# An attention and routed-FFN layer: GpSimd's program follows a planned order, the maxima are turned right behind their split, and the head-term scratch has another layout

## The chip, the cores and the metric

The kernel runs on one core of a Trainium2 chip. Time is device microseconds (us) of one execution, median over several runs; lower is better. Engines: PE (TensorE, matmuls), DVE (VectorE), ACT (ScalarE), POOL (GpSimd) and SP (SyncE, which here issues every DMA).

## What is computed

Input x is 4 batches (B) of T = 1024 tokens of D = 256 values. Both branches read the same layer-normalised x, and their results are added to x:

```python
xn = _layernorm(x)
x = x + attn(xn) + ffn(xn)

# attn: 16 heads of 16 values, causal
q, k, v = split_heads(xn @ Wq.T + bq), split_heads(xn @ Wk.T + bk), split_heads(xn @ Wv.T + bv)
q, k = rope(q), rope(k)
att = where(tril, einsum('bhqd,bhkd->bhqk', q, k) / 4, -inf)
y = softmax(att) @ v                 # then y @ Wo.T + bo
# ffn: 16 blocks of 64 hidden units, each token keeps the 4 blocks with the highest router score
h = relu(einsum('nd,ibd->nib', xf, w1b) + b1b), zero outside the 4 blocks
y = h @ w2.T + b2
```

## The kernel before

**Tiling.** Heads are taken in 16 groups (GROUPS; group n is batch n // 4, four heads each). A group's scores come in 12 units of 128 keys by up to 512 queries, for each of the 4 heads. Everything that PE makes goes through seven rotating PSUM banks (`banks`); the eighth (`o_bank`) holds the sums of probability times value.

**Precision.** Queries and keys are float32, cut into three bfloat16 pieces (high, mid, low). Six products of pieces (NTERM) times 16 values make 96 rows, the "stack" `q_st`/`k_st` of a group. A piece lies with heads on partitions, a stack with terms and values on partitions, so SP writes the pieces to DRAM (`term_scratch`, lines 587 to 621) and reads them back as stacks (lines 607 to 634). Three stacks rotate.

**Maxima.** For each row of scores PE first makes the scores once for their maximum ("max", line 1043), DVE reduces them (lines 1311 and 1314), and for each half of the queries of a group GpSimd cuts the negated maxima into three pieces ("split", `split_maxima`, lines 797 to 806). PE then transposes them ("maxT", the turn, line 1050), DVE copies the result (line 1323), and SP writes it to DRAM and loads it as three extra rows of `q_st` (`place_maxima`, lines 643 and 645). The scores proper ("score", lines 1102 and 1105) of that half need these rows; ACT takes their exponential (line 919). So each half of a group goes: last max on PE, DVE, split on GpSimd, turn on PE, DVE, two DMAs, first score.

**Rotation of queries and keys.** For batch 0 the first two of four projections (r = 0, 1) are rotated and cut by DVE and ACT (lines 1252 to 1275). All later ones, "chains" (b, r), are GpSimd's: `rotate_and_split` issues seven operations of 128x1024 (sin, cos, add, high, rest, mid, low; lines 749 to 776). `high` waits until the pieces of the chain before on the same buffers have been stored. GpSimd also adds the output bias to the accumulator tile (`add_biases`, line 812) and normalises x of the next batches (line 783).

**Order.** Each engine runs its own list in order and waits on semaphores. The lists of PE, ACT and DVE come from one planner (`arrange`): it keeps a clock in matmul columns and models when banks come free and when ACT and DVE are ready. It doesn't model GpSimd in the kernel before. There the turn of a half is placed by a count of maxima (`turned_maxima`, line 125: 24 maxima after the last of a first half, 12 after that of a second), and its scores a fixed 24,000 columns after the last max was read. GpSimd's list is written out by hand (lines 827 to 856), with whole chains between the splits. SP's list is by hand as well (lines 669 to 741).

**The start.** DVE normalises x of batch 0, then copies the value bias, spread over 128 columns, into `bv_wide` (line 1410) and makes the first rotations. GpSimd fills the constant rows of `k_st` (line 819). The first stack load needs all pieces of the first four heads of r = 0 and 1 in DRAM; the pieces of the other heads are stored after it (`store_other_pieces`, line 604), and the second stack load, of group 1, waits for these.

## Time and profile before

| what | us |
|---|---|
| median of 3 runs (lowest, highest) | 854.6 (854.21, 854.64) |
| the profiled execution | 853.66 |
| its span from first to last instruction | 851.9 |
| PE busy in that span | 816.7 |
| DVE, ACT, POOL busy | 591.8, 426.9, 281.6 |

The profile is of one execution. "Busy" of PE counts the time in which any matmul is in flight, so it isn't the share of its peak. A view's "idle before" is the time in which an engine had nothing to run ahead of an instruction, and the arrow names what ended it.

### The profile page before, as it was taken

Reading aid. Unit: us, or ns where it says so; the run is one execution under the profiler, and the core shown is the slowest. Engines: PE = TensorE matmul, PEld = TensorE weight load, DVE = VectorE, ACT = ScalarE, POOL = GpSimd, SP = SyncE. Lnnn points to the kernel's source line nnn. Section 1 sums busy time; section 2 is a strip of 40 time slices with the busy share of each in tenths; the row PEclk is TensorE's granted clock in tenths of the full one; section 3 lists DMA queues with packets and bytes.
Section 4 is the critical chain, followed back from the end, with each engine's and each line's share of the span. In section 5 each row is a group of like instructions: output and inputs, shape, how many; then the busy total and the mean of one; then the engine's idle time right before and its main releaser. Section 6 shows DMA issues by size and latency. Waiting matters only on the chain.

```text
span 851.9 us, 14875 instructions
## 1 busy us (share of the span) xinstructions
PE 816.7 (96%) x5278; PEld 494.4 (58%) x5278; DVE 591.8 (69%) x1800; ACT 426.9 (50%) x1018; POOL 281.6 (33%) x298
## 2 busy tenths in 40 slices
PE   5784999999999999999999999999999999999998
PEld 4463745554546555664766565565666656465664
DVE  7993887868799856667687766767566876668312
ACT  2410355556565554645564464555456554456462
POOL 3155451926344029406515007706250103000000
PEclk9987999999999999999999999999999999999999
DMA  7445331523251445131251414324242224200021
GB/s 261 165 147 153 106 89 52 163 88 100 77 181 34 113 137 164 57 109 36 77 172 42 105 40 135 110 76 101 75 115 100 49 72 142 54 3 26 3 69 50
DMA packets 52375, 81.91 MB, mean 96 GB/s; under 512 B 5836, under 2 KB 21132, under 8 KB 52300
## 3 DMA queue, kind: packets, MB, share of 16 engines
q1 hardware_dynamic: 52300, 80.95, 31.8%
q8 instruction: 42, 0.69, 0.4%
q14 instruction: 33, 0.27, 0.1%
HBM read 43.06 MB, written 37.88 MB: 95 GB/s over the span
## 4 chain that ended last, share of the span: by engine, by line
PE 85%; DVE 4%; ACT 3%; issue 3%; SPq 2%; DMA 2%; POOL 1%; ACTq 0%; DVEq 0%; POOLq 0%
PE o_bank L1118 15%; PE banks L1043 14%; PE banks L1102 14%; PE banks L1031 12%; PE banks L1018 12%; PE banks L992 5%; PE banks L1105 3%; PE banks L1070 3%; ACT probs L919 3%; PE banks L1001 3%; PE banks L1022 2%; DVE o_norm L1410 1%; DMA bv_sb<-in_bv 1%; DMA term_scratch<-pieces 1%; SPq L604 1%
## 5 line engine op out<-in xcount | busy, mean ns | idle before, releaser
L919 ACT ACTIVATE probs<-banks 128x512 f32<-128x512 f32 (+3 forms) x768 | 328.3, 497 | 247.9 <-PE banks L1105 174.3
L1102 PE MATMUL banks<-q_st,k_st 99*128 99x512 bf16 (+3 forms) x768 | 237.1, 328 | 3.4 <-ACT probs L919 0.8
L1043 PE MATMUL banks<-k_st,q_st 96*128 96x512 bf16 (+3 forms) x768 | 229.0, 328 | 1.5 <-issue 0.8
L1314 DVE CUSTOM_DVE_ANT_0 banks<-banks,tri,part_max 128x512 f32<-128x512 f32 (+3 forms) x256 | 129.7, 554 | 72.6 <-PE banks L1043 41.8
L1311 DVE TENSOR_REDUCE part_max<-banks 128x1 f32<-128x512 f32 x256 | 159.6, 680 | 16.3 <-PE banks L1043 15.7
L1314 DVE CUSTOM_DVE_ANT_0 banks<-banks,tri 128x512 f32<-128x512 f32 (+3 forms) x256 | 120.2, 516 | 30.6 <-PE banks L1043 29.1
L1018 PE MATMUL banks<-xnT,w_sb 128*128 128x256 f32 x512 | 137.6, 392 | 0.7 <-ACT probs L919 0.4
L797 POOL TENSOR_SCALAR max_neg<-row_max 128x16 f32<-128x16 f32 x32 | 8.1, 253 | 384.2 <-DVE row_max L1314 384.2
L1118 PE MATMUL o_bank<-probs,v_sb 128*17 128x512 f32 (+3 forms) x1536 | 133.2, 487 | 0.0
L1031 PE MATMUL banks<-w_sb,hT 128*128 128x256 f32 x512 | 121.2, 383 | 0.2 <-DVE row_max L1314 0.2
L1043 PEld LDWEIGHTS banks<-k_st,q_st 96*128 96x128 bf16 x768 | 73.5, 98 | 72.7 <-issue 21.4
L1102 PEld LDWEIGHTS banks<-q_st,k_st 99*128 99x128 bf16 x768 | 74.7, 97 | 62.7 <-ACT probs L919 21.4
L910 ACT ACTIVATE hT<-banks,b_sb 128x256 f32<-128x256 f32 x128 | 60.7, 474 | 97.3 <-PE banks L1022 82.1
L1105 PE MATMUL banks<-identb,tri 128*128 128x128 bf16 x512 | 109.1, 220 | 0.0
L1018 PEld LDWEIGHTS banks<-xnT,w_sb 128*128 128x128 f32 x512 | 92.8, 194 | 25.0 <-issue 3.6
L1031 PEld LDWEIGHTS banks<-w_sb,hT 128*128 128x128 f32 x512 | 94.6, 190 | 16.7 <-DVE row_max L1314 0.7
L1118 PEld LDWEIGHTS o_bank<-probs,v_sb 128*17 128x17 f32 x1536 | 40.1, 97 | 87.2 <-issue 66.8
L1314 DVE DVE_READ_ACCUMULATOR2_ANT row_max<- 128x1 f32 x512 | 71.9, 140 | 0.0
L1105 PEld LDWEIGHTS banks<-identb,tri 128*128 128x128 bf16 x512 | 50.3, 98 | 20.1 <-issue 1.0
L1341 DVE STREAM_TRANSPOSE o_bank<-o_bank 128x512 f32<-128x512 f32 x31 | 22.7, 731 | 44.5 <-PE o_bank L1118 44.5
L1329 DVE TENSOR_TENSOR acc<-acc,banks 128x256 f32<-128x256 f32 x32 | 13.5, 421 | 45.3 <-PE banks L1031 45.3
L749 POOL TENSOR_TENSOR rope_sb<-rope_sb,sin_sb 128x1024 f32<-128x1024 f32 x14 | 33.0, 2354 | 24.4 <-DVE rope_sb L1250 24.3
(97 smaller groups left out, 748.4 us busy)
## 6 DMA issues: line engine op xcount, KB each, us to landing
term_scratch<-pieces SPq DMA_DIRECT2D x84, 256.0 KB
q_st<-term_scratch SPq DMA_DIRECT2D x16, 768.0 KB, 6.9
k_st<-term_scratch SPq DMA_DIRECT2D x16, 768.0 KB, 9.0
y_scratch<-o_norm SPq DMA_DIRECT2D x31, 256.0 KB, 2.5
acc<-in_x SPq DMA_DIRECT2D x8, 512.0 KB, 4.4
rope_sb<-y_scratch SPq DMA_DIRECT2D x15, 256.0 KB
out<-acc SPq DMA_DIRECT2D x7, 512.0 KB, 3.0
x_sb<-in_x SPq DMA_DIRECT2D x3, 1024.0 KB, 7.2
```

The source lines that it names most:

```text
L749: nc.gpsimd.tensor_tensor(y2, y2, sin_sb[:], ALU.mult).then_inc(rotated, 1)
L910: nc.scalar.activation(hT[:, m, :], filled("hid", b, q, m)[:, 0:QTR], ACT.Relu, bias=b1_sb[:, m:m + 1]).then_inc(s_out, 1)
L919: nc.scalar.activation(probs[:, h, PROBS_AT[u]:PROBS_AT[u] + w], filled("score", n, k, h)[:, 0:w], ACT.Exp, scale=SCALE).then_inc(s_out, 1)
L992: last = nc.tensor.matmul(bank, w[:, k, mb * P:(mb + 1) * P], xnT[:, b % 2, k, c * HALF:(c + 1) * HALF], start=(k == 0), stop=(k == KB - 1))
L1018: nc.tensor.matmul(bank[:, 0:QTR], w1_sb[:, k, m * P:(m + 1) * P], xnT[:, b % 2, k, tokens], start=(k == 0), stop=False)
L1031: last = nc.tensor.matmul(bank[:, 0:D], hT[:, m, t % 2 * P:(t % 2 + 1) * P], w2_sb[:, m, :], start=(m == 0), stop=(m == FB - 1))
L1043: nc.tensor.matmul(bank[:, 0:w], q_st[0:KROWS, at, h, i * P:(i + 1) * P], k_st[0:KROWS, at, h, c * HALF:c * HALF + w], start=True, stop=Tr ...
L1102: last = nc.tensor.matmul(bank[:, 0:w], k_st[0:SROWS, at, h, j * P:(j + 1) * P], q_st[0:SROWS, at, h, q0:q0 + w], start=True, stop=not dia ...
L1105: last = nc.tensor.matmul(bank[:, 0:P], tri_k, identb[:], start=False, stop=True)
L1118: last = nc.tensor.matmul(o_bank[h * OW:h * OW + VW, q0:HALF], v_sb[:, b % 2, j, g * GH + h, :], probs[:, h, PROBS_AT[u]:PROBS_AT[u] + HAL ...
L1311: ins = nc.vector.tensor_reduce(part_max[:, h, at:at + 1], bank[:, 0:w], AX.X, ALU.max)
L1314: ins = nc.vector.tensor_tensor_reduce(bank[:, 0:w], bank[:, 0:w], tri[:, HALF - w:HALF], 1.0, least, ALU.add, ALU.max, to)
```

## The change

GpSimd enters the planner. `POOL` lists what each of its operations costs in columns, `pump` runs them on the planner's clock, a split before anything else that is ready, chains one operation at a time, and the resulting list `POOL_ORDER` is what GpSimd executes. A turn is now placed once the planner holds its split to be done (`split[...]`, 1,200 columns after it), and the scores 16,000 columns after the turn. Further:

- The rotations (sin, cos, add) of both chains of batch 0, (0, 2) and (0, 3), go ahead of the first split, and their cutting behind it.
- The copy into `bv_wide` moves from DVE to GpSimd, behind the fill of `k_st`.
- DVE's layer-norm statistics of batch 1 (`ln_stats`, `ln_factors`) leave the start and become chores in group 0.
- `term_scratch` is laid out heads, values, terms, tokens instead of heads, terms, values, tokens. The rows of a stack are then (value, term) in both operands. A store is written as 64 or 128 rows instead of 4x16 or 8x16.
- SP places the first maxima before it stores the pieces of (0, 2), and the second ones before those of (0, 3).

```diff
-def turned_maxima():
-    return [(n * NU * GH + (NU * GH + (12 if n else 5) if half else 16 + (24 if n else 4)), n, half) for n in range(GROUPS)
-            for half in range(2)]
...
+SPLIT, PLACE = 1200, 16000
+POOL = {"split": 3600, "sin": 5640, "cos": 5640, "add": 5640, "high": 2500, "rest": 5100, "mid": 2500,
+        "low": 5100, "xn": 1580, "bias": 5700}
+CHAIN = ("sin", "cos", "add", "high", "rest", "mid", "low")
+RELOAD = 60000
...
-NORMALISED = {3: 2, 7: 3}
+SPLIT, PLACE = 1200, 16000
+POOL = {"split": 3600, "sin": 5640, "cos": 5640, "add": 5640, "high": 2500, "rest": 5100, "mid": 2500,
+        "low": 5100, "xn": 1580, "bias": 5700}
+CHAIN = ("sin", "cos", "add", "high", "rest", "mid", "low")
+RELOAD = 60000
+NORMALISED = {0: 1, 3: 2, 7: 3}
...
+    def pool_work(ready, *works):
+        pool_todo.extend((ready, what) for what in works)
+    def pump():
+        nonlocal pool_free
+        while pool_todo and pool_free <= clock:
+            able = [todo for todo in pool_todo if todo[0] <= clock]
+            if not able:
+                return
+            todo = min(able, key=lambda todo: todo[1][0] != "split")
+            pool_todo.remove(todo)
+            pool.append(todo[1])
+            pool_free = max(pool_free, todo[0]) + POOL[todo[1][0]]
+            if todo[1][0] == "split":
+                split[todo[1][1:]] = pool_free + SPLIT
...
-        placed[maxed] = ready["vector"] + 24000
+        n, k = (maxed - 1) // (NU * GH), (maxed - 1) % (NU * GH) + 1
+        if k in (4 * GH, NU * GH):
+            pool_work(ready["vector"], ("split", n, 0 if k == 4 * GH else 1))
...
+        if what[0] == "out" and what[1] + 1 < B and what[2] % 2:
+            pool_work(ready["vector"] + RELOAD, ("bias", what[1] + 1, what[2] // 2))
...
+        if what[0] == "turn":
+            pool_work(ready["vector"], *((step,) + what[1:] for step in CHAIN))
+        elif what[0] == "newton" and not any(chore[2] == what for chore in chores):
+            pool_work(ready["vector"], *(("xn", what[1], t) for t in range(NT)))
...
-        count, n, half = to_turn[0] if to_turn else (0, GROUPS, 0)
-        return n < GROUPS and (maxed >= count or maxed == len(maxima) and scored >= (GROUPS - 1) * NU * GH + 6)
+        return bool(to_turn) and split.get(to_turn[0], clock + 1) <= clock
     def do_turn():
         work = to_turn.pop(0)
-        do_work([("maxT",) + work[1:]])
-        turned.append(work[1:])
+        do_work([("maxT",) + work])
+        placed[work] = ready["vector"] + PLACE
...
-        if k in (0, 4) and ((n, k // 4) not in turned or placed[n * NU * GH + (48 if k else 16)] > clock):
+        if k in (0, 4) and placed.get((n, k // 4), clock + 1) > clock:
...
+    pool_work(clock + 40000, *((step, 0, r) for r in (2, 3) for step in CHAIN[3:]))
...
+            def term_rows(b, r, t):
+                return term_scratch[b % 2, r, :, :, t].rearrange("c d n -> (c d) n")
...
-                            sp.dma_start(term_scratch[0, r, 0:GH, t], pieces[0:GH * HD, r, piece, :]).then_inc(
+                            sp.dma_start(term_rows(0, r, t)[0:GH * HD], pieces[0:GH * HD, r, piece, :]).then_inc(
...
-                    sp.dma_start(stack[0:KROWS, 0], heads.rearrange("c t d n -> (t d) c n")).then_inc(stacked[0], 16)
+                    sp.dma_start(stack[0:KROWS, 0], heads.rearrange("c d t n -> (d t) c n")).then_inc(stacked[0], 16)
...
+            place_maxima(0, 0)
             store_pieces(0, 2)
-            place_maxima(0, 0)
-            store_pieces(0, 3)
             for b in range(B):
                 n = b * NG
                 more = b + 1 < B
                 place_maxima(n, 1)
+                if b == 0:
+                    store_pieces(0, 3)
...
+            def rotate(step, b, r):
                 y, y2 = rope_pair(r)
-                pool.wait_ge(turned, chain(b, r))
-                nc.gpsimd.tensor_tensor(y2, y2, sin_sb[:], ALU.mult).then_inc(rotated, 1)
-                nc.gpsimd.tensor_tensor(y, y, cos_sb[:], ALU.mult).then_inc(rotated, 1)
-            def low_piece(b, r):
-                pool.wait_ge(mid_done, chain(b, r))
-                _, y2 = rope_pair(r)
-                nc.gpsimd.tensor_tensor(pieces[:, r % 2, 2, :], y2, pieces[:, r % 2, 1, :],
-                                        ALU.subtract).then_inc(low_done, 1)
-            def rotate_and_split(b, r):
+                if step == "sin":
+                    pool.wait_ge(turned, chain(b, r))
+                    nc.gpsimd.tensor_tensor(y2, y2, sin_sb[:], ALU.mult).then_inc(rotated, 1)
+                elif step == "cos":
+                    nc.gpsimd.tensor_tensor(y, y, cos_sb[:], ALU.mult).then_inc(rotated, 1)
+                else:
+                    pool.wait_ge(rotated, chain(b, r) * 2)
+                    nc.gpsimd.tensor_tensor(y, y, y2, ALU.add).then_inc(roped, 1)
...
+            pool.wait_ge(bias_in, 16 * 5)
+            nc.gpsimd.tensor_copy(bv_wide, bv_sb[:, :, None].broadcast_to([P, KB, P])).then_inc(bv_spread, 1)
...
-            rotate_and_split(0, 2)
-            split_maxima(0, 0)
-            rotate_and_split(0, 3)
-            for b in range(B):
-                n = b * NG
-                more = b + 1 < B
-                split_maxima(n, 1)
-                split_maxima(n + 1, 0)
-                if b == 0:
-                    normalise_x(1)
-                split_maxima(n + 1, 1)
...
+            for r in (2, 3):
+                for step in CHAIN[0:3]:
+                    rotate(step, 0, r)
+            for what in POOL_ORDER:
+                if what[0] == "split":
+                    split_maxima(*what[1:])
+                elif what[0] == "xn":
+                    normalise_x(*what[1:])
+                elif what[0] == "bias":
+                    add_biases(*what[1:])
+                elif what[0] in CHAIN[0:3]:
+                    rotate(*what)
+                else:
+                    split(*what)
...
-            dve.wait_ge(bias_in, 16 * 5)
-            nc.vector.tensor_copy(bv_wide, bv_sb[:, :, None].broadcast_to([P, KB, P])).then_inc(bv_spread, 1)
...
-            ln_stats(1, *range(NT))
-            ln_factors(0, NT)
...
-    pieces = nc.dram_tensor("term_scratch", [2, 4, P // HD, NTERM, HD, T], BF16, kind="Internal").ap()
+    pieces = nc.dram_tensor("term_scratch", [2, 4, P // HD, HD, NTERM, T], BF16, kind="Internal").ap()
```

GpSimd's program near its start, before (L749, L750, L764 are sin, cos, add; L772 to L755 the cutting; L797 to L806 the split of the first maxima; L812 the bias):

```order
L819 MEMSET k_st 32x12288
L823 ISA
L823 TENSOR_TENSOR bo_sb<-bo_sb,o_norm 128x256
L812 TENSOR_TENSOR acc<-acc,bo_sb 128x1024 x2
L749 TENSOR_TENSOR rope_sb<-rope_sb,sin_sb 128x1024
L750 TENSOR_TENSOR rope_sb<-rope_sb,cos_sb 128x1024
L764 TENSOR_TENSOR rope_sb<-rope_sb 128x1024
L772 CAST pieces<-rope_sb 128x1024
L774 TENSOR_TENSOR rope_sb<-rope_sb,pieces 128x1024
L776 CAST pieces<-rope_sb 128x1024
L755 TENSOR_TENSOR pieces<-rope_sb,pieces 128x1024
L797 TENSOR_SCALAR max_neg<-row_max 128x16
```

The same place of the changed kernel (L786, L788, L791 are sin, cos, add, L832 is the first step of the split, L805 is `high`):

```order
L854 MEMSET k_st 32x12288
L857 COPY o_norm<-bv_sb 128x256
L860 ISA
L860 TENSOR_TENSOR bo_sb<-bo_sb,o_norm 128x256
L847 TENSOR_TENSOR acc<-acc,bo_sb 128x1024 x2
L786 TENSOR_TENSOR rope_sb<-rope_sb,sin_sb 128x1024
L788 TENSOR_TENSOR rope_sb<-rope_sb,cos_sb 128x1024
L791 TENSOR_TENSOR rope_sb<-rope_sb 128x1024
L786 TENSOR_TENSOR rope_sb<-rope_sb,sin_sb 128x1024
L788 TENSOR_TENSOR rope_sb<-rope_sb,cos_sb 128x1024
L791 TENSOR_TENSOR rope_sb<-rope_sb 128x1024
L832 TENSOR_SCALAR max_neg<-row_max 128x16
```

The cutting of (0, 2) stood before the first split and now stands behind it; three rotations of (0, 3) and the copy came in.

SP's program from the first stores to the second maxima, before:

```order
L597 DMA term_scratch<-pieces 4x16x1024 x12
L612 DMA q_st<-term_scratch 96x4x1024
L612 DMA k_st<-term_scratch 96x4x1024
L604 DMA term_scratch<-pieces 4x16x1024 x12
L634 DMA q_st<-term_scratch 96x4x1024
L634 DMA k_st<-term_scratch 96x4x1024
L620 DMA term_scratch<-pieces 8x16x1024 x6
L643 DMA max_scratch<-max_pcT 48x128
L645 DMA q_st<-max_scratch 3x4x512
L620 DMA term_scratch<-pieces 8x16x1024 x6
```

And after:

```order
L632 DMA term_scratch<-pieces 64x1024 x12
L647 DMA q_st<-term_scratch 96x4x1024
L647 DMA k_st<-term_scratch 96x4x1024
L639 DMA term_scratch<-pieces 64x1024 x12
L669 DMA q_st<-term_scratch 96x4x1024
L669 DMA k_st<-term_scratch 96x4x1024
L678 DMA max_scratch<-max_pcT 48x128
L680 DMA q_st<-max_scratch 3x4x512
L655 DMA term_scratch<-pieces 128x1024 x6
```

The maxima changed places with the six stores of (0, 2), and a store lost its outer dimension of 4 or 8.

PE's program around the turn of the first half of group 1, before (L1043 max, L1102 and L1105 score, L1031 the second FFN product, L1050 the turn); the last max of that half stands 40 rows earlier:

```order
L1043 MATMUL banks<-k_st,q_st 128x384
L1031 MATMUL banks<-w_sb,hT 128x256 x4
L1043 MATMUL banks<-k_st,q_st 128x256
L1031 MATMUL banks<-w_sb,hT 128x256 x4
L1050 MATMUL banks<-identb,max_pc 128x128
```

After (L1065 max, L1124 score, L1072 the turn); the last max of the half is in the first row:

```order
L1065 MATMUL banks<-k_st,q_st 128x128 x3
L1065 MATMUL banks<-k_st,q_st 128x512 x3
L1124 MATMUL banks<-q_st,k_st 128x512
L1065 MATMUL banks<-k_st,q_st 128x512
L1124 MATMUL banks<-q_st,k_st 128x512
L1065 MATMUL banks<-k_st,q_st 128x512
L1124 MATMUL banks<-q_st,k_st 128x512 x2
L1065 MATMUL banks<-k_st,q_st 128x512
L1124 MATMUL banks<-q_st,k_st 128x512
L1065 MATMUL banks<-k_st,q_st 128x512
L1072 MATMUL banks<-identb,max_pc 128x128
```

The turn moved from far behind its last max to 13 matmuls behind it.

## Rows read from the trace of the kernel before

**Rows 1.** The page: the span, and busy time, share and instructions of each engine.

```profile
span 851.9 us, 14875 instructions
PE 816.7 (96%) x5278; PEld 494.4 (58%) x5278; DVE 591.8 (69%) x1800; ACT 426.9 (50%) x1018; POOL 281.6 (33%) x298
```

**Rows 2.** Busy time by stretches: PE, PEld, DVE, ACT, POOL, clock, DMA share, GB/s.

```profile
25.00:50.00 25.00, 18.95 (x63) 11.70 (x62) 23.51 (x68) 11.30 (x31) 5.40 (x4) 0.86 0.43 137
...
75.00:100.00 25.00, 19.73 (x92) 13.92 (x93) 14.97 (x38) 5.20 (x11) 18.04 (x15) 0.82 0.58 172
...
100.00:825.00 725.00, 719.34 (x4817) 429.03 (x4816) 509.40 (x1567) 392.01 (x937) 236.58 (x269) 1.00 0.30 87
```

**Rows 3.** Instructions in time, POOL, DVE, ACT: start, us, engine, line, operation, [idle before].

```profile
14.77 10.33 POOL L819 MEMSET k_st<- 32x12288 bf16 x1 [12.61 <-DVE x_sb L1241]
17.25 8.00 DVE L1410 COPY o_norm<-bv_sb 128x256 f32<-128x256 f32 x1 [2.54 <-DMA bv_sb<-in_bv]
20.89 0.69 ACT L896 ACTIVATE rope_sb<-banks,bqk_sb 128x512 f32<-128x512 f32 x1 [2.08 <-PE banks L992]
27.87 0.72 DVE L1257 STREAM_SHUFFLE rope_sb<-rope_sb 128x512 f32<-128x512 f32 x1
40.62 0.69 DVE L1274 TENSOR_TENSOR pieces<-rope_sb,pieces 128x512 bf16<-128x512 f32 x1 [0.17 <-ACT pieces L877]
```

**Rows 4.** The same view: a DVE operation beside one of POOL.

```profile
54.79 2.36 POOL L764 TENSOR_TENSOR rope_sb<-rope_sb 128x1024 f32<-128x1024 f32 x1
54.99 2.19 DVE L1227 TENSOR_TENSOR square<-rstd 128x8 f32<-128x8 f32 x1
```

**Rows 5.** The chain of work that ended last, in time, around the first stack.

```profile
43.68 6.87 DMA term_scratch<-pieces
50.57 0.32 SPq L612
```

**Rows 6.** Waits of the DMA queue's issuer; stretches as in rows 2; one DMA of the page.

```profile
SPq L634 <- DMA term_scratch<-pieces: 10.2, 1, 10.2
...
62.00:72.00 10.00, 7.47 (x41) 5.65 (x39) 7.31 (x29) 1.42 (x3) 0.00 (x0) 1.00 0.25 95
90.20:99.60 9.40, 9.40 (x51) 6.80 (x50) 7.53 (x26) 2.83 (x6) 3.50 (x3) 1.00 0.45 147
...
k_st<-term_scratch SPq DMA_DIRECT2D x16, 768.0 KB, 9.0
y_scratch<-o_norm SPq DMA_DIRECT2D x31, 256.0 KB, 2.5
```

**Rows 7.** Instructions in time, PE, from the routing mask to the first score.

```profile
44.21 1.01 PE L1010 MATMUL banks<-identb,unsel 128*16 128x128 bf16 x8 [3.59 <-issue]
50.48 1.03 PE L1018 MATMUL banks<-xnT,w_sb 128*128 128x256 f32 x4
56.36 1.02 PE L1043 MATMUL banks<-k_st,q_st 96*128 96x512 bf16 x4 [0.84 <-issue]
80.27 0.29 PE L1050 MATMUL banks<-identb,max_pc 128*128 128x128 bf16 x1 [10.80 <-POOL max_pc L806]
80.35 2.02 PE L1018 MATMUL banks<-xnT,w_sb 128*128 128x256 f32 x4
84.05 1.03 PE L1018 MATMUL banks<-xnT,w_sb 128*128 128x256 f32 x4
94.33 0.38 PE L1102 MATMUL banks<-q_st,k_st 99*128 99x512 bf16 x1
```

**Rows 8.** The same for POOL, around the first split.

```profile
72.32 1.04 POOL L772 CAST pieces<-rope_sb 128x1024 bf16<-128x1024 f32 x1 [15.17 <-issue]
78.83 0.26 POOL L797 TENSOR_SCALAR max_neg<-row_max 128x16 f32<-128x16 f32 x1
```

**Rows 9.** The same: last max of group 5 on PE, last step of its split.

```profile
308.20 0.22 PE L1043 MATMUL banks<-k_st,q_st 96*128 96x128 bf16 x1
...
310.24 0.22 POOL L806 TENSOR_TENSOR max_pc<-max_rest,max_pc 128x16 bf16<-128x16 f32 x1
```

85 lines of the change are left out of this document (37 added, 48 removed).

## The prediction

> **What bounds the kernel now.** I read the page first, then the busy time by stretches, then the instructions in time, and the waits of SP. PE is busy for 816.7 of 851.9 us [rows 1], and between 100 and 825 us it is busy for 719.34 of 725 [rows 2]: there the kernel is PE's own work, and a change that moves POOL's instructions can save at most the 5.7 us that are left. So what can be won lies before 100 us. The reader should see three losses of PE there [rows 7]: 3.59 us before it turns the routing mask at 44.21, 0.84 us before the first max at 56.36, and 10.80 us before the first turn at 80.27, which ends only when POOL has made its split. After the first and the third, TensorE's granted clock is at the lower of its two levels (1.2 instead of 2.4 GHz) for a while: 0.86 and 0.82 on the mean of the two stretches [rows 2], and a group of four hidden-layer matmuls takes 2.02 us at 80.35 where it takes 1.03 at 84.05 [rows 7].
>
> From the first score at 94.33 on, all of the program's long rest follows in PE's order without a gap. My sum is therefore: by how much does the first score come earlier, and what does the rest lose or win against its 757.6 us (851.9 less 94.33).
>
> **The bias copy leaves DVE.** DVE's copy runs from 17.25 to 25.25, just until POOL's fill of k_st ends (14.77 plus 10.33, 25.10) [rows 3]. The copy has 256 elements per partition; it doesn't work for 8 us, it waits for the fill. Everything that DVE, ACT and SP do for the first stack stands behind it. Without it the first rotation can start when its projection is there. The second rotation, of the other 512 columns, then starts when ACT has written its half, at 20.89 + 0.69 = 21.58, and no longer at 27.87 [rows 3]. That is 6.3 us. From there DVE worked without a gap that counts until 41.31 (40.62 + 0.69), ACT's steps between follow DVE's, so the whole stretch moves. I take off 0.1 for the copy's new place: on POOL, at about 25.1, it reads SBUF beside DVE's rotations, and a DVE operation can be held by a POOL one, as the 2.19 us of an operation on 8 columns show, which ended just as POOL's at 54.79 did [rows 4]; at most one 0.7 us operation is held so. **Term a: 6.2 us** (bounds 5.6 and 6.3), if DVE's rotations aren't themselves held by the fill; the first rival takes the other case. PE then has the projections behind each other without the gaps that ACT made, and reaches the mask's turn at 44.21 - 6.2 = 38.0, nearly without the 3.59 us of idle time.
>
> **The clock at 44 us and the first stack.** From 50.48 five of eight hidden tiles take 5.04 us until PE waits at 55.52, 1.01 each. The mask's turn and the three tiles ahead of them took 6.27 (44.21 to 50.48) [rows 7], at full clock 3 x 1.01 + 0.5 = 3.5. If the idle time ahead is nearly gone, the clock should not fall: 2.8 us. The 0.84 us behind the tiles are a wait for the first stack. It must now be there at 38.0 + 8.6 = 46.6, against 56.36. By shift alone it would be there at 50.1. But the stores get quicker: with nothing else in the queue the DMA engines were busy for 0.25 of the time from 62 to 72 us while 64-row stores drained, and 0.45 at 90 to 99.6 with 128-row stores [rows 6]. A quarter and a half of 16 engines: a store of 4x16 rows goes over 4 of them and one of 8x16 over 8. Stores of 64 and 128 rows, as in the new layout, have no such outer dimension, and the stores of o_norm, 128 rows, land in 2.5 us [rows 6]. The last piece store, issued at 43.68, took 6.87 [rows 5]; shifted and with 2.5 us its end is at 35.2 + 2.5 = 37.7, the k_st load is issued then, and lands 5.8 us later (50.57 to 56.36 [rows 5, 7]), at 43.5. That is 3.1 us before PE wants it. **Term b: 2.8 + 0.8 = 3.6 us** (bounds 0 and 3.6).
>
> The Trainium skill (DMA: Bandwidth & Descriptors, Why a DMA increments its semaphore by 16 and not by 1) says that a copy is split over the largest number of engines up to 16 that divides the outermost size of both sides. By that the old stores take 4 and 8 engines and the new ones 16; the trace's 0.25 and 0.45 agree. Without the rule the row of o_norm gives the same price.
>
> **The first turn.** Before, the split waited for (0, 2) to be cut, and `high` waited 15.17 us until all other pieces were stored [rows 8], SP seeing the same as 10.2 us [rows 6]. Now POOL has only the six rotations ahead of the split. Three of them ended at 57.15 (54.79 + 2.36) [rows 4], now at 51.0, and three more of 2.36 each give 58.0. PE's last of the 16 maxima stands some 2 us of work ahead of the place where it waited, 11.1 us behind the first, now at 57.7, and the split starts 0.9 us behind a last max and is done 2.26 us behind it (308.20 to 310.46) [rows 9]: 60.0. PE worked 13.1 us from its first max to the wait (56.36 to 69.47 [rows 7]), and the turn now stands two maxima and a hidden tile, 1.4 us, later: 46.6 + 14.5 = 61.1. It finds its split done, with 1 us to spare. The 10.80 us go, and with them the lower clock after them: 80.27 to 84.05 ran at half, 1.9 us. **Term c: 12.7 us.** If POOL were late after all, it is late by its overrun alone, some 1 or 2 us.
>
> What is late next: the extra rows. SP sends them after the stores of the other pieces (12 issues from 38.1, landed before 50) and the second stack's load, so its queue is empty at 61.6. Two DMAs of 12 KB at 2.5 us each give 66.6, and the first score stands 12.1 us of PE's work behind the turn (80.27 to 94.33, less the 1.9): 46.6 + 13.1 + 12.1 = 71.8. Covered by 5 us. First score 22.5 us earlier.
>
> **The rest.** DVE's layer-norm work of batch 1, 6 to 10 us, is now beside the scores of group 0; DVE is idle for 215.6 of the 725 us after 100 [rows 2], so I count it at nothing, with 2 us as its bound. The layout costs the loads nothing: 96x4x1024 either way. SP stores (0, 3) behind the second maxima; the load that waits for it, group 2's, has over 10 us to spare. The 31 other turns are new: a turn stood some 40 rows behind its last max and now stands 2.6 to 6 us of PE's work behind it, where the split needs 2.3 [rows 9]. That holds when POOL is free. **Term d:** I take 1.3 us lost in all (bounds 0 and 8; a turn that meets POOL in a step of a chain can wait 2.36 [rows 4]).
>
> **Sum.** a + b + c - d = 6.2 + 3.6 + 12.7 - 1.3 = 21.2 us. The span becomes 830.7, the profiled execution 853.66 - 21.2 = 832.5, and the median of 854.6, which lies 0.9 above the profiled one, becomes 833.4.
>
> **Rivals.**
>
> *The rotations are held by the fill as the copy was.* The trace has no DVE operation with two SBUF inputs beside a POOL memset; the copy was held by one, and the operation at 54.99 by a POOL operation that reads. Then the first multiplication, ready at about 17, waits until 25.1, the first rotation ends at 27.1 instead of 27.9, and a is 0.9. The idle time ahead of the mask's turn and the lower clock stay, so b is 0.8; c stays: 0.9 + 0.8 + 12.7 - 1.3 = 13.1, 841.5 us. Neither row is the same case: the one is a copy beside a fill, in the other both operations read, and a fill reads nothing. So I take the free case for the forecast; the trace can't decide. The Trainium skill (SBUF — State Buffer, Who interferes with whom) says that a DVE operation with two SBUF inputs meets only those of GpSimd that read SBUF, and that a copy in a two-port mode meets any. By that rule a is 6.2, and no run here shows it yet.
>
> *The stores don't get quicker*, because rows 12 KB apart land slower than rows side by side, or are issued no faster. Then the second stack's load waits as before, to 72.2 - 6.2 = 66.0, the extra rows queue behind its 9.0 us [rows 6] and land at 77.9; PE, which had its first stack at 50.1, waits 2.6 us there and loses 1 to the clock. First score at 78.9, 15.4 earlier; less d, 14.1: 840.5 us.
>
> *Slower: the tight turns.* Each of the 31 turns stops PE, which has nothing else it may do in order. POOL's steps of 2.36 us can't be broken off, and its list is fixed, so a chain that starts late pushes each split behind it. At a mean wait of 0.7 us per turn the gain is gone; at 1 us the time is 854.6 - 22.5 + 31 = 863. For it speaks that PE has almost no idle time to give. Against it: POOL is busy for 33% [rows 1], and in the old order its splits mostly found it idle.
>
> *The change does what it says, but DVE is short in group 0*: all of the 7 us that moved comes back as waits of PE: 854.6 - 22.5 + 7 = 839.1 us.
>
> **How the numbers follow.** The forecast has 0.60, the held rotations 0.14, the slow stores 0.10, the short DVE 0.08, the tight turns 0.05, and 0.03 stays for less. The time is that of the forecast, 833.4. The range goes from 831.0 (d at nothing, and 1 us of the 5.7 idle ones) to 842.0, which takes in the held rotations and the slow stores and leaves out the tight turns. A difference of 0.2% (1.7 us) is about what a measurement can tell from none. Only the tight turns reach the other side: faster 0.94, same 0.01, slower 0.05.
>
> **What would show it.** In the profile after: DVE's second rotation at about 21.6; a DMA share near 1 instead of 0.25 while piece stores drain; the first max at 46 to 47 and the mean clock of 25 to 50 us at 1.00; the first turn at 61 without a wait on POOL; the first score near 72. Then the sum of PE's waits at turns after 100 us, which is term d. Wrong would be: a rotation that starts at 17 and ends behind 25 (first rival), a k_st load issued behind 42 (second), or waits of PE for max_pc of more than 0.1 us on the mean (third).

## The result and the profile after

The changed kernel takes **830.6 us** (median of 4 runs, 829.97 to 830.82), where the kernel before took 854.6 beside it (854.21 to 854.70). The ratio is 0.9719, 95% interval 0.9702 to 0.9735: 24.0 us less, where I had forecast 21.2 (833.4) and a range from 831.0 to 842.0. The time lies 0.4 us under the low end of that range. The profiled execution took 829.97 us with a span of 828.1.

From the page of the profile after (busy time, share, instructions), and busy time by stretches (us, then PE, PEld, DVE, ACT, POOL, granted clock, DMA share, GB/s):

```profile
span 828.1 us, 14880 instructions
PE 809.9 (98%) x5278; PEld 492.0 (59%) x5278; DVE 579.3 (70%) x1799; ACT 426.2 (51%) x1018; POOL 281.5 (34%) x299
```

```profile
25.00:50.00 25.00, 24.45 (x107) 16.90 (x106) 18.31 (x58) 11.48 (x31) 12.86 (x8) 1.00 0.81 228
75.00:100.00 25.00, 24.47 (x153) 14.37 (x151) 21.35 (x85) 13.31 (x32) 2.17 (x10) 1.00 0.44 128
100.00:801.00 701.00, 695.87 (x4672) 416.89 (x4671) 493.60 (x1515) 377.78 (x906) 234.03 (x259) 1.00 0.29 87
```

Against [rows 1, 2]: the granted clock is 1.00 in all stretches, where 0.86 and 0.82 stood. PE's idle time fell from 35.2 to 18.2 us of the span, and its busy time from 816.7 to 809.9. Most of these 6.8 us are matmuls that no longer run at the lower clock; about 1.1 us are the quicker matmuls ahead of 12 us, of which more is said below. Behind 100 us PE idles for 5.1 us, as before (5.7). So all that was won lies ahead of 100 us, as forecast.

The instructions in time, POOL and DVE, while the fill of k_st runs:

```profile
14.84 10.33 POOL L854 MEMSET k_st<- 32x12288 bf16 x1 [12.68 <-DVE x_sb L1263]
15.27 0.73 DVE L1279 STREAM_SHUFFLE rope_sb<-rope_sb 128x512 f32<-128x512 f32 x1
16.04 0.69 DVE L1280 TENSOR_TENSOR rope_sb<-rope_sb,sin_sb 128x512 f32<-128x512 f32 x1
20.62 0.72 DVE L1279 STREAM_SHUFFLE rope_sb<-rope_sb 128x512 f32<-128x512 f32 x1
25.23 0.41 POOL L857 COPY o_norm<-bv_sb 128x256 f32<-128x256 f32 x1
25.30 0.88 DVE L1281 TENSOR_TENSOR rope_sb<-rope_sb,cos_sb 128x512 f32<-128x512 f32 x1
```

Beside the fill that held the copy for 8.00 us [rows 3], rotations with two inputs take 0.69 us. Only the one beside POOL's copy took 0.88. The shuffles have a single input, and at 0.72 and 0.73 us they aren't held by the fill either. The same view of PE and POOL, from the mask's turn to the first score:

```profile
21.41 7.50 PE L1023 MATMUL banks<-wv_sb,xnT 128*128 128x272 f32 x32
...
37.19 0.61 PE L1032 MATMUL banks<-identb,unsel 128*16 128x128 bf16 x8 [0.55 <-issue]
...
45.63 1.03 PE L1065 MATMUL banks<-k_st,q_st 96*128 96x512 bf16 x4
...
54.79 2.35 POOL L791 TENSOR_TENSOR rope_sb<-rope_sb 128x1024 f32<-128x1024 f32 x1
...
57.66 0.26 POOL L832 TENSOR_SCALAR max_neg<-row_max 128x16 f32<-128x16 f32 x1 [0.52 <-DVE row_max L1336]
...
59.98 0.22 PE L1072 MATMUL banks<-identb,max_pc 128*128 128x128 bf16 x1
...
70.75 0.38 PE L1124 MATMUL banks<-q_st,k_st 99*128 99x512 bf16 x1
```

These answer to [rows 7, 8]: of the three losses 3.59, 0.84 and 10.80 us the first is 0.55, the others are gone. The DMA queue, and busy time while the second dozen of stores drains:

```profile
37.61 0.32 SPq L647 DMA_DIRECT2D k_st<-term_scratch  x1
37.98 8.52 SPq L639 DMA_DIRECT2D term_scratch<-pieces  x12
49.47 0.31 SPq L669 DMA_DIRECT2D q_st<-term_scratch  x1
```

```profile
38.10:49.40 11.30, 11.30 (x58) 8.89 (x57) 6.13 (x15) 3.78 (x8) 11.14 (x6) 1.00 0.88 267
```

The second stack's load is issued at 49.5 instead of 72.2 us, and the DMA share is 0.88 where it was 0.25 [rows 6].

### The profile page after: what moved, and what is told of

Read it like the earlier page. It is cut to its first block, busy times and chain, and to the rows that moved or that the text cites. A ratio compares the mean times of both kernels' runs of the same rounds, so it can differ in the third digit from the quotient of the medians.

```text
span 828.1 us, 14880 instructions
## 1 busy us (share of the span) xinstructions
PE 809.9 (98%) x5278; PEld 492.0 (59%) x5278; DVE 579.3 (70%) x1799; ACT 426.2 (51%) x1018; POOL 281.5 (34%) x299
## 4 chain that ended last, share of the span: by engine, by line
PE 92%; DVE 4%; ACT 2%; issue 1%; DMA 1%; SPq 0%; ACTq 0%; DVEq 0%
PE o_bank L1140 16%; PE banks L1065 14%; PE banks L1124 14%; PE banks L1040 14%; PE banks L1053 14%; PE banks L1014 7%; PE banks L1127 3%; PE banks L1023 3%; PE banks L1092 3%; PE banks L1044 2%; ACT probs L941 2%; DVE part_max L1333 1%; PE banks L1004 1%; DVE o_norm L1370 1%; DVE o_bank L1363 1%
## 5 line engine op out<-in xcount | busy, mean ns | idle before, releaser
L1124 PE MATMUL banks<-q_st,k_st 99*128 99x512 bf16 (+3 forms) x768 | 234.7, 327 | 2.6 <-ACT probs L941 1.0
L1065 PE MATMUL banks<-k_st,q_st 96*128 96x512 bf16 (+3 forms) x768 | 228.7, 327 | 0.7 <-DVE part_max L1333 0.2
L1333 DVE TENSOR_REDUCE part_max<-banks 128x1 f32<-128x512 f32 x256 | 160.1, 679 | 17.6 <-PE banks L1065 17.1
L832 POOL TENSOR_SCALAR max_neg<-row_max 128x16 f32<-128x16 f32 x32 | 8.1, 253 | 382.6 <-DVE row_max L1336 382.6
L1040 PE MATMUL banks<-xnT,w_sb 128*128 128x256 f32 x512 | 134.5, 386 | 0.1
L1065 PEld LDWEIGHTS banks<-k_st,q_st 96*128 96x128 bf16 x768 | 73.3, 98 | 73.9 <-issue 19.9
L1124 PEld LDWEIGHTS banks<-q_st,k_st 99*128 99x128 bf16 x768 | 74.6, 97 | 61.4 <-ACT probs L941 18.1
L1040 PEld LDWEIGHTS banks<-xnT,w_sb 128*128 128x128 f32 x512 | 90.7, 189 | 23.1 <-issue 2.8
L1336 DVE DVE_READ_ACCUMULATOR2_ANT row_max<- 128x1 f32 x512 | 72.2, 141 | 0.0
L786 POOL TENSOR_TENSOR rope_sb<-rope_sb,sin_sb 128x1024 f32<-128x1024 f32 x14 | 33.0, 2357 | 34.7 <-DVE rope_sb L1272 34.7
```

What stands on the lines that cost most here:

```text
L786: nc.gpsimd.tensor_tensor(y2, y2, sin_sb[:], ALU.mult).then_inc(rotated, 1)
L1040: nc.tensor.matmul(bank[:, 0:QTR], w1_sb[:, k, m * P:(m + 1) * P], xnT[:, b % 2, k, tokens], start=(k == 0), stop=False)
L1065: nc.tensor.matmul(bank[:, 0:w], q_st[0:KROWS, at, h, i * P:(i + 1) * P], k_st[0:KROWS, at, h, c * HALF:c * HALF + w], start=True, stop=Tr ...
L1124: last = nc.tensor.matmul(bank[:, 0:w], k_st[0:SROWS, at, h, j * P:(j + 1) * P], q_st[0:SROWS, at, h, q0:q0 + w], start=True, stop=not dia ...
L1333: ins = nc.vector.tensor_reduce(part_max[:, h, at:at + 1], bank[:, 0:w], AX.X, ALU.max)
L1336: ins = nc.vector.tensor_tensor_reduce(bank[:, 0:w], bank[:, 0:w], tri[:, HALF - w:HALF], 1.0, least, ALU.add, ALU.max, to)
```

## What moved the time, in one table

From every trace I read three instants of PE: the start of the value tiles (the row at 21.41 above; nothing that PE does ahead of it is changed), the first score (the row at 70.75), and the end of the span. *To the score* is the second less the first, *rest* is the span less the second. These three columns are of one profiled execution each; in five kernels whose PE has one and the same order (before, copy_alone, layout_alone, split_alone, three_parts) the rest agrees within 0.2 us. The ratio is to the kernel before as it ran beside each kernel, which gave medians of 854.0 to 854.8 us.

| kernel | median us | ratio to before (95%) | value tiles | to the score | rest |
|---|---|---|---|---|---|
| before | 854.0 to 854.8 | | 22.40 | 71.93 | 757.6 |
| changed | 830.6 | 0.9719 (0.9702 to 0.9735) | 21.41 | 49.34 | 757.4 |
| copy_back | 838.8 | 0.9822 (0.9807 to 0.9837) | 22.44 | 57.00 | 757.6 |
| copy_two_inputs | 831.4 | 0.9733 (0.9718 to 0.9747) | 23.12 | 49.14 | 757.5 |
| old_layout | 838.6 | 0.9822 (0.9807 to 0.9837) | 23.16 | 56.62 | 757.3 |
| late_split | 836.9 | 0.9805 (0.9789 to 0.9821) | 21.25 | 55.84 | 757.3 |
| copy_alone | 848.1 | 0.9924 (0.9910 to 0.9939) | 22.43 | 67.29 | 757.4 |
| layout_alone | 847.9 | 0.9921 (0.9905 to 0.9938) | 22.37 | 65.98 | 757.6 |
| split_alone | 849.3 | 0.9939 (0.9924 to 0.9954) | 22.26 | 68.48 | 757.6 |
| three_parts | 843.1 | 0.9864 (0.9849 to 0.9879) | 21.40 | 61.90 | 757.4 |
| norm_early | 839.6 | 0.9830 (0.9810 to 0.9849) | 21.31 | 61.11 | 754.5 |
| norm_alone | 856.2 | 1.0024 (1.0014 to 1.0035) | 21.53 | 73.42 | 759.9 |
| four_parts | 833.1 | 0.9755 (0.9737 to 0.9774) | 22.17 | 49.80 | 759.2 |
| old_turns | 834.2 | 0.9769 (0.9747 to 0.9790) | 21.70 | 50.16 | 760.2 |
| norm_unheld | 827.5 | 0.9683 (0.9669 to 0.9696) | 22.21 | 49.25 | 754.4 |
| stats_early | 828.2 | 0.9690 (0.9677 to 0.9703) | 22.09 | 49.19 | 755.1 |
| warm_early | 828.5 | 0.9696 (0.9683 to 0.9709) | 20.01 | 49.65 | 757.3 |
| both_early | 825.7 | 0.9674 (0.9661 to 0.9687) | 19.79 | 49.34 | 754.5 |

The value tiles begin anywhere from 21.25 to 23.16 us in kernels whose PE has the same work up to there (all but the last two). The copy, the layout and the first split move the second column alone. Two things move the third by more than 0.3 us: where DVE makes batch 1's statistics, which moves the second as well, and where the turns stand. Undone one by one (copy_back, old_layout, late_split, norm_early, old_turns), the five parts cost 8.2, 8.0, 6.3, 9.0 and 3.6 us, 35 together for a change that won 24: they share waits.

## The experiments

**One part of the changed kernel undone.** First the copy, at its old place on DVE, in two forms:

```diff
+            dve.wait_ge(bias_in, 16 * 5)
+            nc.vector.tensor_copy(bv_wide, bv_sb[:, :, None].broadcast_to([P, KB, P])).then_inc(bv_spread, 1)
             first_rotation(0, 0)
```

> The changed kernel with one part undone: the spreading copy of the bias stands on DVE again, ahead of the first rotation. Theory (the copy is held by GpSimd's fill of k_st until about 25.2 us, as in the kernel before): the copy takes about 8 us, the second rotation starts near 27 instead of 20.6, the first max comes 7 to 8.5 us later and the idle time ahead of the mask's turn is back; 838.6 us (837 to 840). Rival (the 8 us were not the fill's doing, and the earlier start of the rotations came from the other parts): the copy takes under 1 us, 831 to 832 us.

```diff
+            bv_cols = bv_sb[:, :, None].broadcast_to([P, KB, P])
+            nc.vector.tensor_tensor(bv_wide, bv_cols, bv_cols, ALU.max).then_inc(bv_spread, 1)
             first_rotation(0, 0)
```

> As copy_back, on the same engine and in the same place, but the spreading is written as a maximum of the bias with itself, so that the DVE operation has two inputs in SBUF and no longer one. Theory (only the copy with one input is held by GpSimd's fill, as the rotations were not): it takes 0.4 to 0.5 us beside the fill and the time is 831 us (830.5 to 832). Rival (any DVE operation that stands there is held, for example because it starts at the same moment as the fill's DMA or reads with a step of zero): it takes about 8 us and the time is 838 to 840 us.

838.8 and 831.4 us. The same 256 elements, in time, from copy_back and then from copy_two_inputs:

```profile
14.74 10.33 POOL L854 MEMSET k_st<- 32x12288 bf16 x1 [12.59 <-DVE x_sb L1261]
19.10 6.12 DVE L1430 COPY o_norm<-bv_sb 128x256 f32<-128x256 f32 x1 [4.42 <-DMA bv_sb<-in_bv]
```

```profile
14.86 10.33 POOL L854 MEMSET k_st<- 32x12288 bf16 x1 [12.70 <-DVE x_sb L1261]
16.47 0.43 DVE L1431 TENSOR_TENSOR o_norm<-bv_sb 128x256 f32<-128x256 f32 x1 [1.67 <-DMA bv_sb<-in_bv]
```

The copy ends with the fill (25.22 against 25.07) though its bias came 1.9 us later than before; with two inputs it isn't held at all. So the fill held it, and by its form, not its place. The Trainium skill (SBUF — State Buffer, Who interferes with whom) says that a DVE operation with two inputs in SBUF meets only those of GpSimd that read it, while a copy in a two-port mode meets any; the traces agree, with 0.43 against 6.12 and 8.00 us. Whether the copy ran in such a mode no trace shows.

Then the layout:

```diff
-                return term_scratch[b % 2, r, :, :, t].rearrange("c d n -> (c d) n")
+                return term_scratch[b % 2, r, :, t]
```

> The changed kernel with the scratch of the terms in its old layout, so that a piece store has an outer dimension of 4 (8) again. Theory (the stores go over 4 or 8 of the 16 engines and drain slowly): the first stack lands 3 to 5 us after PE wants it, the second stack's load waits until about 65 us and the extra rows behind it, DMA share 0.25 while stores drain; first score near 78, 837.5 us (835 to 841). Rival (in the new order the queue has room enough and the layout is worth nothing, or only the 0.8 us of the first stack): 831 to 832 us.

838.6 us. PE waits 4.48 us for the first stack, and the next loads go out at 67.17 instead of 49.47:

```profile
51.83 1.44 PE L1065 MATMUL banks<-k_st,q_st 96*128 96x512 bf16 x3 [4.48 <-issue]
```

```profile
52.00:62.00 10.00, 10.00 (x36) 7.36 (x35) 5.64 (x18) 0.00 (x0) 6.59 (x3) 0.72 0.26 102
```

The DMA share is 0.26 again while stores of 4x16 rows drain, and the granted clock falls behind PE's wait (0.72 on the mean of these 10 us). The Trainium skill (DMA: Bandwidth & Descriptors, Why a DMA increments its semaphore by 16 and not by 1) would have 4 of 16 engines; the trace agrees, and so does the 0.88 of the new layout.

Then the order of the first split:

```diff
+            for step in CHAIN[3:]:
+                split(step, 0, 2)
             for what in POOL_ORDER:
+                if what[1:] == (0, 2) and what[0] in CHAIN:
+                    continue
...
-            place_maxima(0, 0)
             store_pieces(0, 2)
+            place_maxima(0, 0)
```

> The changed kernel with GpSimd cutting (0, 2) ahead of the first split again, and SP storing its pieces ahead of the first maxima's rows; PE's order as in the changed kernel. Theory 1 (the early split carries all of term c): PE waits about 10.8 us at the first turn and loses 1.9 to the clock, 843 us. Theory 2 (the stores of the new layout have long been done by then, so that the cutting costs its own four steps of 6.3 us and no more): PE waits 5 to 5.5 us at the first turn and the clock costs 0 to 2, 836 to 838 us. Theory 2 would mean that the layout and the early split each remove the same half of the old wait.

836.9 us, as the second theory had it:

```profile
64.77 0.29 PE L1076 MATMUL banks<-identb,max_pc 128*128 128x128 bf16 x1 [4.90 <-POOL max_pc L841]
```

```profile
64.50:68.00 3.50, 3.23 (x9) 2.04 (x10) 1.10 (x3) 0.47 (x1) 3.36 (x4) 0.51 0.13 47
```

POOL cuts (0, 2) without a wait at 56.81, where `high` had waited 15.17 us [rows 8]. Its four steps of cutting delay the split by 5.7 us (63.33 instead of 57.66), PE waits 4.90, and the granted clock is at its lower level behind the wait (0.51 in the row above). So behind the new layout the early split is worth 6.5 us to the score, 4.9 of wait and the rest mostly clock, and not the 12.7 of my term c: the other half of that old wait were the slow stores, which the layout takes away by itself.

**One part alone on the kernel before.** copy_alone moves the copy, layout_alone changes the layout, and split_alone has

```diff
-            rotate_and_split(0, 2)
             split_maxima(0, 0)
-            rotate_and_split(0, 3)
+            split(0, 2)
+            split(0, 3)
```

with both rotations ahead of it and SP's first maxima ahead of its stores of (0, 2). three_parts has all three.

> The kernel before with one part of the change: the spreading copy of the bias goes from DVE to GpSimd, behind the fill. Theory (DVE's chain comes 6.3 to 7 us earlier, and the stores, the first split and the first turn follow it, so that PE still waits about 10 us at that turn): 6.6 us won, 847.6 us (847.0 to 848.5). Rival (the clock fall of 2.8 us is won on top, since PE's idle time ahead of the mask's turn goes): 844.8 us.

> The kernel before with one part of the change: the scratch of the terms in the new layout. Theory (the wait of GpSimd's high step for the stores was most of the first turn's delay): high of (0, 2) starts near 58.5 instead of 72.3 us, the first turn comes at about 69 with less than 1 us of wait, first score near 81, 841.2 us (840.5 to 843). Rival (only the first stack's 0.8 us is won and the cutting ahead of the split still sets the turn): 850 to 853.5 us.

> The kernel before with one part of the change: GpSimd makes both rotations and the first split ahead of the cutting of (0, 2), and SP sends the first maxima's rows ahead of the pieces of (0, 2). Theory (the turn is free at about 70 us, but the extra rows queue behind the second stack's load, which waits for the slow stores until 72.2): first score near 84.5, 844.8 us (843.5 to 846.5). Rival (the slow stores don't matter once the split is early): first score at 82.1, 842.3 us or less.

> The kernel before with all three parts (copy on GpSimd, new layout, early first split), but PE's and DVE's order as before: the turns where they stood, and DVE's layer-norm statistics of batch 1 ahead of the first maxima. Theory (the planner's moves behind the first turn are worth nothing): 830.6 us (829.8 to 831.8). Rival 1 (the counted places of the turns win something): 832.5 us or more. Rival 2 (the tight turns and the moved statistics cost the 1.3 us that were forecast): 829.3 us or less.

They came to 848.1, 847.9, 849.3 and 843.1 us. Only the first time was as I expected, and not its make-up: PE waits 4.51 us for its first stack and 7.68 at its first turn, where I had about 10 at the turn. Alone the three won 6.8, 7.0 and 5.5 us. Together they won 11.8, where it should have been the whole gain. What is late in three_parts, DVE and POOL in time and one PE row:

```profile
43.58 0.64 DVE L1230 BATCH_NORM_AGGREGATE mv<-stats 128x2 f32<-128x6 f32 x8
44.25 1.14 DVE L1232 TENSOR_SCALAR var<-mv 128x8 f32<-128x8 f32 x1
45.42 2.28 DVE L1237 TENSOR_SCALAR guess<-var 128x8 int32<-128x8 int32 x1
47.73 0.17 DVE L1238 TENSOR_SCALAR rstd<-guess 128x8 int32<-128x8 int32 x1
47.94 2.20 DVE L1244 TENSOR_TENSOR square<-rstd 128x8 f32<-128x8 f32 x1
50.17 2.26 DVE L1245 SCALAR_TENSOR_TENSOR square<-square,var 128x8 f32<-128x8 f32 x1
...
54.77 0.17 DVE L1244 TENSOR_TENSOR square<-rstd 128x8 f32<-128x8 f32 x1
...
58.00 0.70 DVE L1331 CUSTOM_DVE_ANT_0 banks<-banks,tri 128x512 f32<-128x512 f32 x1
```

```profile
47.74 2.37 POOL L767 TENSOR_TENSOR rope_sb<-rope_sb 128x1024 f32<-128x1024 f32 x1
50.07 2.34 POOL L753 TENSOR_TENSOR rope_sb<-rope_sb,sin_sb 128x1024 f32<-128x1024 f32 x1
...
54.79 2.35 POOL L767 TENSOR_TENSOR rope_sb<-rope_sb 128x1024 f32<-128x1024 f32 x1
```

```profile
58.82 1.15 PE L1060 MATMUL banks<-k_st,q_st 96*128 96x384 bf16 x2 [8.21 <-DVE row_max L1331]
```

The first max of PE is at 45.80, but DVE takes none before 58.00. It is still in the block of statistics of batch 1. Of its twelve small operations of 0.17 us, eight begin while POOL rotates: five of them take 2.2 to 2.3 us, until POOL's step ends, one takes 1.14, and two that begin in the instant between two steps (47.73 and 54.77) take 0.17. The last four stand behind POOL's rotations. The block stood in the same place in the kernel before. But there the first max came only at 56.36, behind three rotations and not six; the block was through at 58.79, and PE waited for nothing of it. layout_alone and split_alone met it too (5.54 and 4.80 us of PE's time on the same release).

**The block, and the turns.** norm_early puts the block back into the changed kernel (and the normalising of batch 1 into GpSimd's list where the planner no longer enters it), norm_alone moves it in the kernel before, and four_parts is three_parts with the block moved. old_turns gives the changed kernel's turns their old counts:

```diff
-NORMALISED = {0: 1, 3: 2, 7: 3}
+NORMALISED = {3: 2, 7: 3}
...
             turn_halves(0, 3)
+            ln_stats(1, *range(NT))
+            ln_factors(0, NT)
```

```diff
-        return bool(to_turn) and split.get(to_turn[0], clock + 1) <= clock
+        if not to_turn:
+            return False
+        count = turned_maxima()[2 * to_turn[0][0] + to_turn[0][1]][0]
+        return maxed >= count or maxed == len(maxima) and scored >= (GROUPS - 1) * NU * GH + 6
```

> The changed kernel with one part undone: DVE makes the layer-norm statistics of batch 1 ahead of the first maxima again. Theory (found in the run with three parts: this block of small operations is held one by one by GpSimd's rotations and then bars DVE from the first maxima): the block starts near 41 and ends near 58 us, PE waits about 8 us for DVE among the first maxima and loses 2 to 3 us to the clock, first score near 83; 842.5 us (841 to 844). Rival (the block costs only its own 6 us of work, most of it hidden, and the run with three parts lost its time elsewhere, in the places of the turns): 831 to 834 us.

> The kernel before with one part of the change: the layer-norm statistics of batch 1 are made by DVE among the scores of group 0. Theory (in the kernel before the block stands beside the wait for the first stack and ends at 58 us, before the late first turn at 80.3 needs anything of it): worth nothing alone, 854.3 us (853.6 to 855.2). Rival (it is worth its time wherever it stands): 848 us or less.

> The kernel before with all three parts of the run three_parts and the statistics moved as well; turns, and GpSimd's order behind the first split, as before. Theory (the four parts together are the whole gain, and the counted order behind the first turn is worth nothing): 830.6 us (829.8 to 832). Rival (the turns right behind their splits, or GpSimd's chains in single steps, win something of their own): 833 us or more.

> The changed kernel with the turns at the counts of maxima at which they stood before, some 30 maxima later than now. Theory (in either place no turn waits for GpSimd): 830.6 us (829.8 to 831.6). Rival 1 (the tight turns cost the 1.3 us of the forecast): 829.3 us or less. Rival 2 (the later turns delay the scores): 832 us or more.

839.6, 856.2, 833.1 and 834.2 us. The first shows the block's price ahead of the first maxima (11.8 us to the score), and most of what each of the four missed my number by stands in the last column of the table. Read it as a square (before and three_parts; norm_early and norm_unheld; norm_alone, four_parts and old_turns; changed):

| rest, us | turns at the old counts | turns behind their splits |
|---|---|---|
| block ahead of the first maxima | 757.6, 757.4 | 754.5, 754.4 |
| block among the scores | 759.9, 759.2, 760.2 | 757.4 |

The block costs 1.8 to 2.9 us among the scores, and the turns behind their splits **win** 1.8 to 3.1. The change does both, and they cancel. In the turns' share are the scores that follow them, since the planner counts these from the turn, and in part GpSimd's planned list; no run takes these apart, and four_parts and old_turns, which share a cell, differ by 1.0 us. Both effects are local, as the first score of some groups shows (us from the first score of group 0, groups counted from 0):

| first score of group | 2 | 4 | 6 | 10 | 15 |
|---|---|---|---|---|---|
| three_parts | 94.3 | 172.7 | 275.2 | 475.3 | 708.1 |
| norm_early | 94.2 | 172.4 | 273.4 | 472.6 | 705.3 |
| four_parts | 96.2 | 174.7 | 277.0 | 477.1 | 709.9 |
| changed | 96.9 | 175.3 | 276.2 | 475.4 | 708.1 |

The block's price (changed less norm_early) is there by group 2, 2.7 of 2.9 us. The turns' gain (three_parts less norm_early) comes from a few groups, 4, 5 and 9 above all, and not evenly from 31 turns. It is seen in the waits of PE's weight loads for a bank that ACT still reads at a score, from the kernel before, four_parts, the changed kernel and norm_early (us in total, times, longest):

```profile
PEld banks L1102 <- ACT probs L919: 21.4, 64, 0.7
```

```profile
PEld banks L1119 <- ACT probs L936: 23.8, 72, 0.7
```

```profile
PEld banks L1124 <- ACT probs L941: 18.1, 57, 0.7
```

```profile
PEld banks L1126 <- ACT probs L943: 17.7, 55, 0.7
```

With the turns behind their splits scores find their bank free more often. They are short waits, under 0.8 us, that mostly don't show as idle time of PE. The block's price is not in this row: norm_early has 17.7 against 18.1, for 2.9 us. Why the one placing meets ACT less often than the other I didn't take apart, so the cause of the turns' gain stays open behind this.

**The causes taken away.** norm_unheld has the block ahead of the first maxima as norm_early does, but POOL out of its way:

```diff
+            pool.wait_ge(ln_step, 2 * LN_STEPS + LN_CHAIN)
+            for step in CHAIN[0:3]:
+                rotate(step, 0, 2)
+            rotate("sin", 0, 3)
             for what in POOL_ORDER:
+                if what == ("high", 0, 2):
+                    rotate("cos", 0, 3)
+                    rotate("add", 0, 3)
```

> As norm_early (the statistics of batch 1 ahead of the first maxima), but GpSimd starts its rotations of (0, 2) only when that block is done, and makes the two last steps of (0, 3) behind the first split. Theory (the small operations were held one by one by GpSimd's rotations, and the statistics among the scores cost about 2.9 us of the rest): the block takes 6 to 7 us instead of 17, PE waits less than 1 us among the first maxima, first turn at about 60, the rest from the first score 754 to 755 us, 827.7 us (827 to 829). Rival (the block is long by itself, 17 us whatever GpSimd does): 839 us or more.

stats_early leaves the eight aggregations and the twelve small operations among the scores:

```diff
-            steps = [("stats", b, t) for t in range(NT)] + ...
+            steps = [("stats", b, t) for t in range(NT if n else 0)] + ...
...
             turn_halves(0, 3)
+            ln_stats(1, *range(NT))
```

> The changed kernel, with the eight statistics operations of 0.42 us ahead of the first maxima and the twelve small ones left among the scores. Theory (these eight are not held by GpSimd and fit in DVE's free time ahead of the first maximum; they are the larger part of what the block costs among the scores): first max as in the changed kernel, 1 to 2 us less from the first score on, 829.1 us (828.4 to 830.2). Rival (the eight are held too, or the cost among the scores comes from the small ones): 830.6 us or more.

827.5 and 828.2 us. In norm_unheld the same operations as in three_parts, and then the first maximum:

```profile
44.25 0.64 DVE L1241 BATCH_NORM_AGGREGATE mv<-stats 128x2 f32<-128x6 f32 x8
...
45.13 0.17 DVE L1248 TENSOR_SCALAR guess<-var 128x8 int32<-128x8 int32 x1
45.34 0.17 DVE L1249 TENSOR_SCALAR rstd<-guess 128x8 int32<-128x8 int32 x1
45.54 0.17 DVE L1255 TENSOR_TENSOR square<-rstd 128x8 f32<-128x8 f32 x1
...
47.34 0.70 DVE L1342 CUSTOM_DVE_ANT_0 banks<-banks,tri 128x512 f32<-128x512 f32 x1
```

The block takes 5.8 us (from 41.53) instead of 17.1 (40.86 to 57.97). So the time was POOL's hold, not the block's length. In stats_early eight of its 28 operations, those of 0.42 us, give back 2.2 of the 2.9 us of the rest. The other 20 also come earlier there (the aggregations at 73.56 instead of 84.10), so the 2.2 aren't the eight operations' price alone.

warm_early tests the start:

```diff
-            pe.wait_ge(ident_in, 16)
+            pe.wait_ge(ones_set, 1)
             for _ in range(WARM):
-                nc.tensor.transpose(banks[:, BANKS - 1, 0:P], ident[:], ident[:])
+                nc.tensor.matmul(banks[:, BANKS - 1, 0:HALF], unselT[:, 0:P], unselT[:, 0:HALF], start=True, stop=True)
+            pe.wait_ge(ident_in, 16)
```

> The changed kernel with its 18 warming matmuls on the identity, which wait for their DMA until about 7 us, replaced by 22 matmuls on a tile that GpSimd has zeroed by 1.7 us. Theory (the granted clock's step up is counted from when PE begins to work, and its varying time, 9.9 us in one trace and 11.8 in another, was the 1.0 us by which the changed kernel started earlier): the clock is up before the first transposition, which starts at about 9.4 us instead of 10.5, 829.4 us (828.6 to 830.2). Rival (DVE's normalisation or a DMA sets that start): 830.6 us.

828.5 us; PE's transpositions start at 9.05 us, now behind a wait of 0.42 for DVE's normalised x, and the value tiles at 20.01, 1.4 us ahead of the changed kernel's. The interval of this kernel and that of stats_early still touch the changed kernel's; it is their columns of the table that tell them apart. both_early joins warm_early with norm_unheld:

> norm_unheld and warm_early together: the statistics of batch 1 ahead of the first maxima with GpSimd's rotations behind them, and the warming matmuls on the zeroed tile. Theory (the two gains lie in different places, the start of PE and the rest behind the first score, and add up): 3.1 and 2.1 us below the changed kernel's 830.6, 825.4 us (824.8 to 826.4). Rival (with PE 1.5 us earlier the block of 6.6 us bars DVE from the first maxima, or GpSimd is late for the first turn, and the second gain is lost): 827 us or more.

825.7 us (825.28 to 827.01), the quickest version by its median, though its interval still touches that of norm_unheld: value tiles at 19.79, and a rest of 754.5. The gains lie in different columns and add up, 4.9 us below the changed kernel where the two alone gave 3.1 and 2.1.

## Why the forecast was right and where it wasn't

**Up to the first score the sum was right.** Counted from the value tiles, the first score came 22.6 us earlier (71.93 less 49.34); the forecast had 22.5. Term by term, with the 1.0 us by which the value tiles themselves were early taken off:

- Term a: the second rotation at 20.62, so 7.25 - 1.0 = 6.3 us; forecast 6.2. The rival of held rotations fell: they took 0.69 us beside the fill.
- Term b: the first max at 45.63 is 10.73 earlier, 9.7 without the start; forecast 9.8 for a and b. The clock stayed at 1.00, and the k_st load went out at 37.61, 38.6 without the start (forecast 37.7). The 35.2 in that sum doesn't follow from its row: 43.68 less 6.2 is 37.5. It holds only if SP issues faster too, which I didn't argue. SP did: it was through with the first twelve stores 1.5 us behind DVE's last piece (35.76 against 34.28), before 3.6 (44.86 against 41.31).
- Term c: the turn at 59.98, without a wait, is 19.3 earlier than before without the start; forecast 19.2. The split was done at 59.05, 60.0 without the start, and I had 60.0; the rotations ended at 57.14, 58.1 without it, and I had 58.0.
- The rival of slow stores fell as well: the share is 0.88.

**Two sizes were off, both to the same side, and the time fell below the range.** Either error alone would have left it inside: 831.6 without the early start, 832.1 with term d as it stood (sums from the figures below). The *start* had no term. I took the profiled execution of before as it was, and its value tiles began at 22.40, those of the changed kernel at 21.41. Rows of PE's first transpositions, before and after:

```profile
10.95 1.71 PE L982 MATMUL banks<-ident,x_sb 128*128 128x128 f32 x8
```

```profile
10.52 1.04 PE L1004 MATMUL banks<-ident,x_sb 128*128 128x128 f32 x8
```

They are the same instructions, 1.71 us against 1.04. The change doesn't touch them, and the value tiles behind them vary by 1.9 us among the table's kernels: 21.53 in norm_alone, whose start is that of the kernel before, and 23.16 in old_layout, whose start is the changed kernel's. That 1.0 us belongs in a range, not in a sum, and my range had no place for it. One trace each can't say how much of it is in the medians.

**The step that failed is term d: 1.3 us lost, where 0.2 were won.** It had two parts, and each was wrong by more than the sum of both. "I count it at nothing" stood for DVE's statistics among the scores: they cost 1.8 to 2.9 us, in groups 0 and 1. The 31 tight turns I priced at a loss, "bounds 0 and 8", so that the range could not reach below them: with the scores that follow them they won 1.8 to 3.1. No turn waits for POOL in the changed kernel. I looked for what the new place can cost, and not for what the old one did. 1.0 for the start, 1.5 here and 0.1 ahead of the first score are the 2.6 by which the span's gain of 23.8 passed the forecast's 21.2. The medians' gain is 24.0. That the two parts nearly cancel, so that d is off by only 1.5, is luck.

**One step was right by luck.** The sum for terms b and c let DVE take the first maxima as soon as PE made them. That holds only because the change also moves the block of statistics, which I had filed under the rest, at nothing. Without it the block ends at 58 us (57.97 in three_parts, 57.75 in norm_early) though the first stack is there by 46, and the gain is 14.6 us (norm_early) and not 24.0. The row at 54.99 [rows 4] had shown the price: I read it as a bound for one operation of the copy's place and not for the block in which it stands. The question what is late next, which I asked of the extra rows, had to be asked of the first max too.

The rivals: DVE short in group 0 was the nearest to what happened (2.9 of its 7 us in the changed kernel); no turn waits for POOL, so that the slower case did not come.

## What to carry to other kernels

When several waits in a row are taken away, write down what each engine does in the window that they covered. Work that was free there becomes the next wait, and parts that win 7, 7 and 5.5 us alone may win 12 together, or 21 with a fourth that alone loses 2 (four_parts). An interaction like that is seen by undoing one part of the finished version and by adding one to the old one; either alone misleads.

Split the trace at instants that keep the causes apart (here the value tiles, the first score and the first score of each group). Differences of 0.3 us become readable that way, where whole times vary by 1 us.
